# A graph layer on one core: the first edge stage moved ahead of the attention, the sort's placing and the scatter

## The reference, cut to what matters

```
xn = layernorm(x)
x1 = x + gat(xn, src, dst) + mix(xn)
out = x1 + experts(layernorm(x1))        # gate: a second graph attention over 131072 edges

gat: h = xn @ W; a_src, a_dst = (h * att).sum per head
     e = leaky_relu(a_src[src] + a_dst[dst]); softmax of e over each dst
     out[dst] += h[src] * weight         # 4 heads of 64
mix: q, k, v = xn @ W_qkv                # 4 heads of 32, one sequence of 6250
     k = softmax over the 6250 nodes; context = k^T v per head
     out = (q * scale) @ context @ W_out + b_out
```

## Time and profile before

| | |
|---|---|
| runs | 4527.89, 4528.56 (median), 4533.54 us |
| the profiled execution | 4524.41 us, its span 4522.3 us |
| attention, sort, scatter | 0 to 464.4 us |
| schedule, until the first gather | 464.4 to 510.6 us |
| edges | 510.6 to 2629.5 us |
| nodes | 2629.5 to 2803.1 us |
| regroup, gating and experts, combination | 2803.1 to 4522.3 us |
| TensorE clock, mean granted | 0.852 |

### The profile page before, as it was taken

How to read it: one execution, slowest core, us unless ns; L and a number is a source line. 1 busy time by engine, 2 the same in 40 slices (tenths; PEclk the granted TensorE clock), 3 DMA queues, 4 the chain that set the end, 5 groups by cost and what they waited for, 6 DMA issues and landing times. The chain is left out here.

```text
span 4522.3 us, 91034 instructions
## 1 busy us (share of the span) xinstructions
PE 3512.5 (78%) x19013; PEld 3030.9 (67%) x19014; DVE 2915.0 (64%) x8563; ACT 1579.3 (35%) x5217; POOL 2876.3 (64%) x2985
## 2 busy tenths in 40 slices
PE   0285588888888888888888825899999999999970
PEld 0273477777777777777777715788888888888860
DVE  8866666666666666666666664566566566555668
ACT  0133233333333333333333343444445444444430
POOL 0417577777777777777777730666666666666650
PEclk9997688888888888888888855899999999999975
DMA  3010133333333333333333441211111111111138
GB/s 97 14 43 6 51 107 107 107 106 107 106 107 106 107 106 107 106 107 106 107 106 107 104 70 10 59 23 26 23 26 26 23 26 24 25 23 25 24 57 244
DMA packets 195040, 323.43 MB, mean 72 GB/s; under 512 B 65331, under 2 KB 114837, under 8 KB 195003
## 3 DMA queue, kind: packets, MB, share of 16 engines
q0 software_dynamic: 121248, 235.98, 22.7%
q1 hardware_dynamic: 65916, 79.03, 6.5%
q10 hardware_dynamic: 7839, 8.03, 0.6%
HBM read 282.42 MB, written 40.40 MB: 71 GB/s over the span
## 5 line engine op out<-in xcount | busy, mean ns | idle before, releaser
L915 POOL DMA_INDIRECT msg<-table,idx x1680 | 1587.8, 945 | 537.4 <-issue 454.3
L1461 POOL DMA_INDIRECT xmsg<-xtable,xidx x1132 | 1069.7, 945 | 475.1 <-issue 327.4
L1069 PE MATMUL psS_e<-msg,hot 128*125 128x260 f32 x3360 | 1125.2, 493 | 153.5 <-issue 147.6
L1069 PEld LDWEIGHTS psS_e<-msg,hot 128*125 128x125 f32 x3360 | 763.6, 238 | 322.8 <-issue 171.0
L1043 PEld LDWEIGHTS psD_e<-ad_m,hotT 125*128 125x128 f32 x3368 | 460.9, 212 | 212.5 <-issue 211.4
L1043 PE MATMUL psD_e<-ad_m,hotT 125*128 x3368 | 469.5, 266 | 171.7 <-DVE lg L1001 171.3
L1007 DVE TENSOR_TENSOR msg<-msg,psW_e 128x1024 f32<-128x1024 f32 x420 | 508.3, 1210 | 0.0
L979 DVE TENSOR_TENSOR room<-room,psS_e 125x260 f32 x842 | 358.1, 425 | 188.7 <-issue 120.8
L949 ACT ACTIVATE psW_e<-lg 128x16 f32<-128x16 f32 x420 | 78.7, 187 | 1020.1 <-DVE lg L1001 1020.1
L1564 DVE TENSOR_TENSOR xprod<-psD_g,xhi 128x160 f32<-128x160 f32 x283 | 91.9, 325 | 501.9 <-PE psD_g L1620 497.0
L996 DVE TENSOR_TENSOR lg<-msg,psD_e 128x16 f32<-128x16 f32 x420 | 72.1, 172 | 497.5 <-DMA msg<-table,idx 492.6
(11 more groups left out here) (330 smaller groups left out, 4712.7 us busy)
## 6 DMA issues: line engine op xcount, KB each, us to landing
msg<-table,idx POOLq DMA_INDIRECT x1680, 2.8
experts_out<-y_room SPq DMA_DIRECT2D x101, 224.0 KB
y_back<-experts_out SPq DMA_DIRECT2D x25, 896.0 KB
xmsg<-xtable,xidx POOLq DMA_INDIRECT x1132, 2.4
table<-hrow SPq DMA_DIRECT2D x50, 113.8 KB
x_all<-in_x SPq DMA_DIRECT2D x5, 1120.0 KB
hs<-table SPq DMA_DIRECT2D x5, 1120.0 KB
out<-x_all ACTq DMA_DIRECT2D x25, 224.0 KB
```

Of the source, the lines that this page charges most:

```text
L915: nc.gpsimd.indirect_dma_start(msg[:, u, j, :], None, table[:, :], bass.IndirectOffsetOnAxis(ap=idx[:, u, j:j + 1], axis=0)).then_inc(gath ...
L1069: last = nc.tensor.matmul(psS[:, u % 2, j // GT, 0:ROW], hot[:, u, j, :], msg[:, u, j, :], start=j % GT == 0, stop=j % GT == GT - 1)
L1461: nc.gpsimd.indirect_dma_start(msg[:, u, j, :], None, xtable[:, :], bass.IndirectOffsetOnAxis(ap=idx[:, u, j:j + 1], axis=0)).then_inc(gat ...
```

## The change

What it does, stage by stage:

1. **`tables`** takes the place of the first two stages. The edge columns and the step list are made beside the projection of h. The attention vectors are folded into W (`w_ext`, 264 columns), so that one matmul gives h and both logits. xn transposed stays in `x_room`. q, k and v are not made here. The 55 rounds of the sort run between the blocks on VectorE (`sort_round`). Then the stage ends, with the sort done and nothing placed.
2. **`edges`** does the same 420 steps, in eight parts (`PARTS`). Between its steps: k's maximum (54 steps), k, v and context block by block (150), the product into `xmix` in HBM (150), the places of the sorted cells (60, unrolled). The results of the inserted matmuls stand in `psD` beside the picked logits; a step's `dst_picked` is given after them. The picked logits come as three bf16 parts (`ad_b`, `hotT` in bf16), which VectorE sums (`look`) before it makes `lg`.
3. **`nodes`** issues the 137 scatters to `xlist` on GpSimd at its start, VectorE adds the messages instead of GpSimd, and `x_all` is read back from `xmix`.

The diff's core:

```diff
+def tables(...):                       # for linear_attention_and_projections and schedule
+    for n in range(2):                 # VectorE
+        ch.link(V.tensor_tensor(wprod, w_ext[:, :, 0:D], bcast(att[:, n, :], 1, KC), ALU.mult))
+        V.reduce_sum(w_ext[:, :, D + n * GH:D + (n + 1) * GH], ...)
+    measure(0); invert(0); normalize(0..2); key casts
+    for n in range(BLOCKS):
+        if n + XN < BLOCKS:
+            normalize(n + XN)
+        if c < XCH and n % XB == 3: measure(c)
+        if c < XCH and n % XB == 5: invert(c)
+        if n == 1: groups_begun()
+        if n == 15: groups_listed()
+        for r in range(rounds * n // BLOCKS, rounds * (n + 1) // BLOCKS):
+            sort_round(nc, ch, r, a[:], b[:])
+    dve.wait_ge(h_kept, 2 * BLOCKS)
+    V.tensor_reduce(top[:], ...).then_inc(top_known, 1)     # GpSimd then shares it
...
 def edges(...):
+    PARTS = (("max", 0, 8), ("max_end", 8, 1), ("context", 9, 25), ("context_end", 34, 1), ("mix", 35, 25),
+             ("places", 60, 5), ("sizes", 65, 1), ("places", 66, 4))
     # TensorE, step k
-    pick(k + 1, u + 1, ...)
+    bs = blocks_of(k + 1)
+    pe.wait_ge(logits, s * STEPS + k + 1)
+    if u in TAKES[part]:
+        pe.wait_ge(part_taken, takes_done(s, part, t, u))
+    picked = pick(bs, u + 1, ...)
+    made = make(s, part, t, u)
+    (made or picked).then_inc(dst_picked, 1)
     # make: max, every 2nd step: 2 matmuls of 250 columns; context, of 3 steps: one with 2 of 256, one that
     # waits for kx_ready and has 1 of 129; mix, of 3 steps: one with 3 of 256
...
     # ScalarE, context, u % 3 == 1, after stage(k + AHEAD)
+    act.wait_ge(ks_ready, ...)
+    nc.scalar.activation(kx[0:NB], ks[:], ACT.Exp).then_inc(kx_ready, 1)
...
     # VectorE, step k
-    ch.link(nc.vector.tensor_tensor(lg[:, u, :, :], msg[:, u, :, D:ROW], pick[:, :, 0:GH], ALU.add))
+    ch.link(V.reduce_sum(look[:], psD[:, 0:BESIDE].rearrange("p (j s f) -> p j f s", j=ST, s=3), AX_X))
+    ch.link(V.tensor_tensor(lg[:, u, :, :], msg[:, u, :, D:ROW], look[:, :, 0:GH], ALU.add))
     ...
     one_hot((u + 3) % SLOTS, ...)
+    take(s, part, t, u)                # the inserted results out of PSUM: 1 or 2 operations of 128 to 256 columns
+    if places is not None:
+        place(s, places, k - PARTS[5][1] * SLOTS)
     dve.wait_ge(weights, ...)
+    # place, n = 0..8: compare 1024 keys, sum 1024; n = 9, 32, 33: chains of 9 to 11 small operations;
+    # n = 35..43: three over 128 to 283; n = 45..53: three over 128, one multiply and one sum over 1024
...
 def nodes(...):                        # GpSimd
-    each_few(pool, sum_messages)
+    for q in range(XQ):
+        scatter(sorted_keys[:, q * XK:(q + 1) * XK], where_i[:, q:q + 1])
+    for g in range(CLASSES - 1):
+        scatter(extra[:, g, :], extra_i[:, g:g + 1])
     pool.wait_ge(top_known, 1)
     nc.gpsimd.partition_all_reduce(topall[:], top[:], NB, RMAX).then_inc(top_shared, 1)
+    pool.wait_ge(scattered, 16 * (XQ + CLASSES - 1))
```

More of the change, by code:

```diff
@@ L219, in build @@
                 sweeps = isb("sweeps", [EP, 1], I32)
[L220 to L236, removed]
+                topall = isb("topall", [NB, GH])
+                key = isb("key", [P, XEP])
+                spare = isb("spare", [P, XEP])
+                at8 = isb("at8", [P, XQ])
+                stepno = isb("stepno", [P, XSTEPS])
@@ L250, in build, with tables @@
         combine(nc, scope, x_all, gate, y_dram, y_sb, y_loaded, out)
[L253 to L256, removed]
+def tables(nc, scope, x, src, dst, W, att_src, att_dst, xedges, table, x_room, ident, ones, zeros, node, agg, sd_all,
+           topall, src_i, dst_f, neg_base, step_group, step_block, sweeps, key, spare, sorted_keys, at8, stepno,
+           tri, unused, row):
     U = 2
+    XN, XU = 3, 4
+    WIDE = D + 2 * GH
     used = []
@@ L819, in _ @@
[L819 to L824 removed]
+            dve.wait_ge(weights_in, 48)
@@ L829, in _ @@
+            v = xedges.rearrange("s (p e) -> s p e", p=P)
+            for a in range(2):
+                act.dma_start(ends[a], v[a]).then_inc(xedges_loaded, 16)
+            for a, to in ((0, dst_f), (1, src_i)):
                 for c in range(CHUNKS):
@@ L865, in edges @@
+    nc.clear_and_free_semaphores(used)
+    nc.all_engine_barrier()
+def edges(nc, scope, x, W_qkv, W_out, b_out, gbias, table, xmix, xlist, x_room, ident, ones, zeros, node, sd_all, ad_b,
+          ex_self, topall, agg, src_i, dst_f, neg_base, step_group, step_block, sweeps, key, spare, sorted_keys, late,
+          at8, stepno, tri, unused, where_i, extra, extra_i, cls_i, row):
     with ExitStack() as ctx:
@@ new lines, in edges @@
+        TAKES = {"max": {1: 1, 3: 1, 5: 1}, "max_end": {1: 1, 3: 1, 4: 1}, "context": {1: 1, 2: 1, 4: 1, 5: 1},
+                 "context_end": {0: MH, 1: 1, 2: 1, 3: 1, 4: 1}, "mix": {1: 1, 4: 1}, "sizes": {1: 1}, "places": {}}
+        assert BLOCKS == 2 * (3 * 8 + 1) == 2 * 25 and TRIPS == 70
+        FIRST_TAKE = {}
+        taken = 0
+        for name, _, trips in PARTS:
+            FIRST_TAKE.setdefault(name, taken)
+            taken += trips * sum(TAKES[name].values())
+        ALL_TAKES = taken
@@ new lines, in _ @@
+            first, up, t1, t2 = [cnt[:, n, :] for n in range(4)]
+            torn, size, steps = [cnt[:, n, 0:CLASSES] for n in (4, 5, 6)]
+            base = cnt[:, 7, :]
+            t3, t4, start, shift = [cnt[:, n, 0:CLASSES] for n in (8, 9, 10, 11)]
+            jump = cnt[:, 12, 0:CLASSES - 1]
+            sum_below, sum_all = cnt[:, 13, 0:CLASSES], cnt[:, 14, 0:CLASSES]
+            dst_keys = sorted_keys[:].bitcast(U16).rearrange("p (n h) -> p n h", h=2)[:, :, 1]
+            PLACE_LINKS = 135
```

1174 lines of the change are left out of this document (613 added, 561 removed).

## The result

The changed kernel takes 4271.1 us (median of 4 runs, 4268.6 to 4273.2) against 4528.9 for the kernel before (4 runs): a ratio of 0.9427, 95% interval 0.9415 to 0.9439. The forecast was 4254, with a range of 4205 to 4335. The profiled execution has a span of 4266.8 us and a mean granted clock of 0.869.

The account below looks back on a forecast made before the run. The prediction took GpSimd's issue of gathers, 5.0 us a step of four, as the bound. It summed 4524.4 - 324.6 (tables) + 33 (edges) + 19 (nodes) = 4251.8 us, forecasting a median of 4254, range 4205 to 4335.

Parts of the forecast that it names:

- four lower bounds: Lowest deviations taken for the terms: tables -16 us, context -10, places and tail -10, nodes -5.
- Tables: Start up to the first gather: VectorE's list sets the length, first gather near 186 us instead of 510.6, -324.6.
- 16 us: In tables: 1.6 MB of edges come first on the load queue and take about 16 us.
- Context and mix at the gathers' pace: In edges: the inserted attention work fits the gathers' pace of 5.0 us a step, costing +10 us over 150 steps.
- 14.4 of 15: In edges: TensorE's work per three context steps takes 14.4 us of the 15 available, so it fits, barely.
- chain of waits: Rival, 0.14: context steps paced by the wait for exp (4334 us), tables by block latency (4298), or both (4380).
- TensorE at 1.2 GHz: Rival, 0.03: TensorE stays at the lower clock through the edge stage, adding 299 us, 4543 in all.
- Places: Places steps in edges: VectorE passes 5.0 us a step, 8.3 in steps 45 to 53, leaving a final lag of 31.
- delays up to 11 us cost nothing: In edges: GpSimd needs a staging some 14 us after the logits, so delays up to 11 us are free if made good.
- lag of 10.6: In places: nine steps and nine small operations put VectorE 10.6 us behind, made good before the next part.
- Port lock: Rival, 0.03: VectorE operations with two SBUF inputs stop the gathers for their own length, 214 us, 4468 in all.
- Nodes: Nodes stage: 137 scatters at 0.996 + 0.30 us take 178 us, the shared maximum stands behind them, +19 us.

Follow-up runs that it names:

- e8: Changed kernel with chunks 2 to 4 of x loaded after the edge extension instead of before: ratio 0.945 to the kernel before, first gather at 178.6 us.
- e9: Changed kernel with places work spread over steps, x chunks 2 to 4 loaded later, maximum shared after 107 scatters, eight scatters moved into edges: 4253.4 us, ratio 0.9397.
- e1: Changed kernel with the picks in fp32 again and the logits read directly from PSUM: ratio 0.954 to the kernel before, on a slow chip.
- e1b: The same kernel as e1, run on another slow chip: ratio 0.956 to the kernel before.
- e6: Changed kernel with den copied to PSUM, so one of three nodes updates has one SBUF operand: ratio within 0.942 to 0.945, scatter stretch 11.6 us.
- e11: Changed kernel with nothing but 64 tiny memsets added on VectorE in nodes: ratio 0.9503 to the kernel before, on a slow chip.
- e5: Changed kernel with the maximum in nodes shared after 107 of the 137 scatters instead of after all: ratio 0.943 to the kernel before, on a slow chip.

## Why the prediction was right, and where its terms were off

- **The total** missed by 17 us (4271 against 4254), inside the range: edges 4.8, nodes 10.2, the rest 2.9, tables -0.8. The sum itself had a slip: 4251.8 and the 4.2 up to the median are 4256, not 4254. And the lower end, 4205, lies below all four lower bounds taken together (41 us less, 4213).
- **Tables** came to within 0.8 us of the forecast, and by the mechanism named: VectorE's list, with GpSimd waiting 163 us for its maximum. That it came so near is luck, since terms inside were off and cancelled. The loads landed 5.4 us later than the "16 us". The edge extension, queued behind x on SyncE, cost a wait of 5.95 that was not in the sum (e8 shows it). The rest of the list was 7.2 shorter than its rows had added up to. So VectorE ended 4.2 late, and sharing the maximum took 0.5 us and not 5.8.
- **Context and mix at the gathers' pace**: right; +10 was twice the measured 5. Even those 5 are the gathers' own duration, 0.948 us and not 0.945, as in the gating stage, which was not edited; in e9 the mix steps run at 5.00. The "14.4 of 15" overstated TensorE: the wait for exp was 0.9 and not 2.1, the clock 0.87 and not 0.82, and VectorE still waited 0.83 us a step for gathers. The rivals of a chain of waits and of TensorE at 1.2 GHz didn't come.
- **Places**: mechanism right, size 23 against 32 (39.0 less 6.9 us of a shorter tail, 13.9 instead of 20.8). The last steps were foreseen at 8.3 us each and took 8.46. What failed is "delays up to 11 us cost nothing": the first thirty steps lost 6.6 us, with the lag of 10.6 that I had let go free.
- **Port lock**: the row that I took against it was fair for what it shows, operations of 0.17 us: e1 and e1b leave about 3 us for it. From the ends measured here that can be understood, as an estimate: 0.17 and 0.82 us are hardly more than a gather's own 0.95. But the rule was dismissed for the long ones as well, and the earlier trace rows had shown one of 3.97 us. The Trainium skill (SBUF — State Buffer, SBUF: two separate sides) says that of a VectorE operation with two SBUF inputs and a GpSimd operation that reads SBUF, the one that starts first has the shared ports for its whole instruction. Where VectorE's started first, the traces agree for operations of 1.5 and 2.0 us, with e6's table and the ends 0.77 and 0.85 us behind VectorE's. The other order did not show with these DMAs: in e6 the addition of 3207.05 began 0.41 us into a scatter and took 1.49 us all the same, as all of its kind did.
- **Nodes**: the all-reduce stood behind the scatters as forecast, but 137 x 1.296 was too little. They took 189.2 us, 12.0 of them stretch beside VectorE's operations: this is the term that was off by 10. The row of 0.996 had been read in another stage, beside other VectorE work.
- **Behind nodes** I left +0; it was +2.9, not explained. e9 and e11 show that an edit ahead of this part can change it.

## What to carry to other kernels

When one engine's issue rate sets the pace, work inserted beside it is free while every step of every other engine fits in a step, and it is worth cutting the work until it does: here 26 of 39 us. Before putting long VectorE operations beside indirect DMAs of GpSimd, look for those with two SBUF operands, and compares like the one above: each can hold one DMA until after it ends. Compare also the stages that an edit doesn't touch, and the packets of the queues that load instructions: in e9, code that had only moved came with 31 us more in such a stage, as much as the edit of the edges gained.

## What the runs showed of the hardware

- An indirect DMA on GpSimd that starts during a long VectorE operation with two fp32 SBUF operands ends about 0.8 us after it: 2.51 us instead of 0.95 beside one of 2.01, and on average 1.22 to 1.65 instead of 0.97 beside ones of 1.49. Beside one SBUF and one PSUM operand it lasts 0.97. A compare of 0.68 us from one 16-bit SBUF tensor does the same (1.44). VectorE's own operation takes no longer for it.
- VectorE stood 2.7 to 3.1 us once per trip of a loop, at one place, after 64 instructions had been put ahead of it. The Trainium skill (Runtime: NRT & Kernel Launch, Instruction fetch mechanics) says that a taken branch whose target is outside the two resident blocks of instructions waits for a fetch. The stalls once per trip agree with it, and so do the five packets per trip on the instruction queue (107 against 0 over 1300 us). How large the blocks are was not measured, and moving the loop by 24 more did not help.
- Three chips ran the kernel before and all variants but e9 about 1.3 times slower (5906 to 6029 us for the kernel before) with the same durations of gathers, 0.947 to 0.952 us, and of VectorE's operations; the kernels nearest to the changed one, e5, e6 and e8, stood at 0.942 to 0.945 of the kernel before. In e5 GpSimd waited for ScalarE's staging up to 6.6 us in steps where in the changed kernel it never waited more than 0.3:

```profile
POOL msg L758 <- ACT rel L773: 269.6, 68, 6.6
```

That is 1700 to 2600 us, steps 221 to 348. The cause of the slower chips was not found; the kernels without the stalls before `xhi` are as slow there and load no more instructions than the changed kernel (53 to 56 packets against 55).
